# Gated weight tables kept in 32 bit, and the cast of x moved to GpSimd

## Chip, cores and metric

The kernel runs on one core of a Trainium2 chip. The metric is the device time of one execution in microseconds (us). A measurement is compared as a ratio against runs of the kernel before on the same chip.

## What is computed

The input x is 16 images of 128 channels and 32 x 32 pixels, taken as 16 batches of 1024 tokens of 128 values. Three layers follow one another:

- a 128 x 128 channel mix with the inverse of a circulant matrix;
- causal linear attention: layer norm, projections to q, k and v, `elu + 1` on q and k, 8 heads of 16, cumulative sums over the tokens, output projection, residual;
- a feed-forward layer whose weights differ from batch to batch. A small gate net turns the mean over a batch's tokens into 8 gate values g, and the weights are merged from a base and 8 task tables.

The parts that the change touches are, from the reference:

```python
gh = jax.nn.relu(jnp.einsum('bsd,hd->bsh', x, gfc1_w) + gfc1_b)
g = (jnp.einsum('bsh,eh->bse', gh, gfc2_w) + gfc2_b).mean(axis=1)
W1m = W1 + jnp.einsum('be,efd->bfd', g, tv_W1)
W2m = W2 + jnp.einsum('be,edf->bdf', g, tv_W2)
h = jax.nn.relu(jnp.einsum('bsd,bfd->bsf', x, W1m) + b1m[:, None, :])
out = jnp.einsum('bsf,bdf->bsd', h, W2m) + b2m[:, None, :]
```

## The kernel before

**Precision.** Most products run in 16 bit with split operands: a value a is stored as a_hi (a cast to f16) and a_lo (a minus a_hi, again f16), and a product is three products, hi x hi, hi x lo and lo x hi, added up in PSUM. So each 32-bit value needs a cast and a subtraction on some engine before TensorE can read it.

**Attention.** The 16 x 1024 tokens are 128 tiles of 128 tokens. All engines run the same software pipeline over slots: in slot s a stage with skew k works on tile s - k. The order of the stages in a slot is written out by hand for each engine (lines 42 to 52), and each engine runs its list in that order, waiting on semaphores. Two batches are unrolled, the others run in a loop of eight slots each (lines 429 to 447). The stages that matter here, with engine and skew:

- x_hi (ScalarE, skew 0, line 722): for the even tile n of a pair, the cast of the 256 columns of tiles n and n+1. The buffers xh and xl hold eight tiles, so the cast overwrites tiles n-8 and n-7 and first waits for their out-projections (`wo_done`).
- x_lo (GpSimd, skew 0, line 1036): the subtraction, after x_hi. In GpSimd's slot it comes after rsqrt (line 977) and z_hi (line 1020) and before z_lo, qk_hi and qk_lo.
- conv (TensorE, skew 0, line 559): needs x_hi and x_lo of its tile. Statistics on VectorE (stats1, mean_var1) follow, then rsqrt on GpSimd with skew 1, and exp_qk and v_hi on ScalarE with skew 1.
- turn_out (TensorE, skew 6, line 654) transposes the attention output after the divide on VectorE (line 907), copy_out on ScalarE brings it back, and out_project (skew 6, line 660) adds x_hi and x_lo products to it and counts `wo_done`.
- scores (skew 4) writes PSUM, scores_hi on ScalarE and scores_lo on VectorE split it, and values (TensorE, skew 5, line 629) reads the split.

TensorE's slot is state, scores, conv, turn_out, values, out_project, gate (every other slot), project.

**The task tables.** tv_W1 and tv_W2 are loaded during attention in 16 shares, one for each batch, from SyncE's queue (line 486) into a small 32-bit buffer. ScalarE casts each share to tv_hi (tv_hi, line 733, four casts of 128 x 128 for each batch), VectorE makes tv_lo (line 844), and the next load waits for that (`tv_split`).

**The merges.** Merged weights of eight batches are made at a time. A bank of PSUM takes four groups; a group is three products of table parts with gate blocks and one with the base weights (lines 1189 to 1192). ScalarE or VectorE casts the bank to its high part and VectorE subtracts the low part. Eight banks of W1 for the first half of the batches are merged in the last slots of attention (merge_w1, line 685), the other eight after attention (lines 1239 to 1243), and 16 for the second half between the two halves of the FFN loop (line 1101). That is 32 banks or 128 groups.

Of the kernel before, what the change touches and what calls it, by code (L numbers as in the profile page):

```python
# [8 lines left out]
F16 = mybir.dt.float16  # L9
BF16 = mybir.dt.bfloat16  # L10
ALU = mybir.AluOpType
# [4 lines left out]
P = 128  # L16
# [13 lines left out]
GB = 8  # L30
# [52 lines left out]
def shape_constants():  # L83
# [3 lines left out]
    def put(name, a):  # L87
        k[:a.shape[0], COL[name][0]:COL[name][1]] = a
# [6 lines left out]
    put("delta", (j[:, None] % FI == np.arange(FI)[None, :]).astype(np.float32))  # L95
# [34 lines left out]
def build(nc, d):  # L130

    top = ExitStack()
    with top:
        def sb(ctx, name, shape, dt=F32):
            return ctx.enter_context(nc.sbuf_tensor(name, shape, dt))
# [25 lines left out]
        tv = [sb(top, f"tv_{s}", [P, 2, FO * C], F16) for s in ("hi", "lo")]  # L161
# [9 lines left out]
        gbf = sb(top, "gate_blocks_f32", [P, GB, FI])  # L171
        gbh = sb(top, "gate_blocks_hi", [P, B, FI], F16)
        gbl = sb(top, "gate_blocks_lo", [P, B, FI], F16)
# [208 lines left out]
        with early, ExitStack() as pa_:  # L382
# [14 lines left out]
            tvs = sb(pa_, "tv_share", [P, 2, TVW])  # L397
# [23 lines left out]
            tv_loaded = [sem(f"tv_loaded_{i}") for i in range(2)]  # L421
            tv_hi_ready, tv_split = sem("tv_hi_ready"), sem("tv_split")
# [17 lines left out]
            def run(eng, order, stages, behind=None):  # L440
# [3 lines left out]
                with eng.Fori(2, B) as b:  # L444
                    batch(stages, b)
                for b in range(B, B + 2):
                    batch(stages, b, behind)
# [4 lines left out]
            TVP = 4  # L452
            MERGE_SLOT = 4

            with nc.Block() as block:
                @block.sync
                def _(sp):
# [28 lines left out]
                    def load_tv(b, t):  # L486
                        if t not in (1, 5) or isinstance(b, int) and b + 1 == B:
                            return
                        which = t // 4
                        sp.wait_ge(ones_set, 1)  # L490
# [3 lines left out]
                    def tv_rows(b, which):  # L494
                        src = (d["L1_ffn_tv_W1"].rearrange("e (i o) d -> (e i) (o d)", i=FI),
                               d["L1_ffn_tv_W2"].rearrange("e (i o) f -> (e i) (o f)", i=FI))[which]
                        sp.dma_start(tvs[:, which, :], src[:, bass.ds(b * TVW, TVW)]).then_inc(tv_loaded[which], 16)
# [12 lines left out]
                    for which in range(2):  # L510
                        tv_rows(0, which)
# [19 lines left out]
                def _(pe):  # L531
# [153 lines left out]
                    def merge_w1(slot):  # L685
# [9 lines left out]
                        if k == 0:  # L695
                            pe.wait_ge(base_placed, 16 * 4)
                            pe.wait_ge(tv_split, TVP * B)
# [3 lines left out]
                        gh, gl = [x[:, 0:GB, :].rearrange("p b i -> p (b i)") for x in (gbh, gbl)]  # L701
# [19 lines left out]
                def _(act):  # L721
                    def split_x(b, t):
                        if t % 2 or isinstance(b, int) and TILES * b + t == 0:
                            return
                        n = TILES * b + t
                        hf, j = t // HALF, t % HALF
                        if j == 0:
                            act.wait_ge(x_loaded[hf], 16 * (b + 1))
# [4 lines left out]
                    def tv_hi(b, t):  # L733
                        if t % 2:
                            return
                        which, part = divmod(t // 2, 2)
                        act.wait_ge(ones_set, 1)
                        act.wait_ge(tv_loaded[which], 16 * (b + 1))
                        nc.scalar.activation(tv[0][:, which, bass.ds(b * TVW + part * TVW // 2, TVW // 2)],
                                             tvs[:, which, part * TVW // 2:(part + 1) * TVW // 2], ACT.Copy, scale=WS)\  # L740
                            .then_inc(tv_hi_ready, 1)

# [82 lines left out]
                    run(act, SCALAR_ORDER, {"tv_hi": tv_hi, "split_x": split_x, "read_t1": read_t1, "v_hi": v_hi,  # L825
# [5 lines left out]
                def _(dve):  # L831
# [11 lines left out]

                    def tv_lo(b, t):
                        if t % 2:
                            return
                        which, part = divmod(t // 2, 2)
                        dve.wait_ge(tv_hi_ready, TVP * b + t // 2 + 1)
                        cols = bass.ds(b * TVW + part * TVW // 2, TVW // 2)
                        nc.vector.scalar_tensor_tensor(tv[1][:, which, cols],  # L850
                                                       tvs[:, which, part * TVW // 2:(part + 1) * TVW // 2], WS,
                                                       tv[0][:, which, cols], ALU.mult, ALU.subtract).then_inc(tv_split, 1)
# [80 lines left out]
                    def merged_w1(slot):  # L933
# [5 lines left out]
                        if slot == MERGE_SLOT - 2:  # L939
# [4 lines left out]
                            nc.vector.tensor_tensor(gbf[:, :, :],  # L944
                                                    kcol("delta").unsqueeze(1).broadcast_to([P, GB, FI]),
                                                    grep[:, 0:GB].unsqueeze(2).broadcast_to([P, GB, FI]), ALU.mult)\
                                .then_inc(gb0_chain, 1)
                            dve.wait_ge(gb0_chain, 2)
                            nc.vector.tensor_copy(gbh[:, 0:GB, :], gbf[:, :, :]).then_inc(gb0_chain, 1)
                            dve.wait_ge(gb0_chain, 3)  # L950
# [528 lines left out]
```

## Time and profile before

| | us |
|---|---|
| median of 3 runs | 747.9 |
| lowest, highest run | 747.24, 750.97 |
| the profiled execution | 749.55 |
| its span (first to last instruction) | 747.8 |
| attention loop, from about | 30 |
| attention loop, to about | 480 |

The granted clock of TensorE is 0.975 of full speed on average. The profile's page gives busy time for each engine, the span in 40 slices and the costliest groups of instructions. A line of a group says: line, engine, operation, output<-inputs, shapes, count, busy time, mean duration in ns, and the idle time before it with what ended it. A line of the timeline says: start, duration, engine, line, operation. Records on one engine can overlap, because the next instruction starts to flow in before the one ahead has written its last result; for matmuls the distance from start to start tells what one costs.

### The profile page before, as it was taken

To read this page: it belongs to the slowest core of one execution; us is meant where nothing else is said; L and a number is where in the kernel's file an instruction comes from. 1 tells how busy PE (TensorE), PEld (TensorE's weight loads), DVE (VectorE), ACT (ScalarE), POOL (GpSimd) and SP (SyncE) were. 2 spreads that over 40 slices of the span, in tenths; PEclk is the share of its full clock that TensorE was granted. 3 is DMA by queue.
4 is the path that set the end of the run, shared out by engine and by line. 5 is a ranking of instruction groups with operands and counts; after the bars stand their busy time and mean duration, and the time that the engine had idled before them with its cause. 6 is when DMAs were issued, how large, how long until landed. Compare 5 with 4: busy or idle time off the path is not lost. (4 is left out here: it accounts for less than half of the span.)

```text
span 747.8 us, 38168 instructions
## 1 busy us (share of the span) xinstructions
PE 692.5 (93%) x12002; PEld 533.8 (71%) x12002; DVE 659.1 (88%) x2409; ACT 649.1 (87%) x1780; POOL 465.2 (62%) x790
## 2 busy tenths in 40 slices
PE   4898899999999999999999999888999998999993
PEld 2576677777777777777777777775777787777772
DVE  5697889999999999999999999768898977998983
ACT  4797989999999999999999999557888876888883
POOL 3686778888888888888888888421333321333333
PEclk9798999999999999999999999899999999999998
DMA  4757676666666666666666666410222211222221
GB/s 149 112 110 134 132 129 129 148 143 131 148 142 132 148 141 132 148 141 134 148 139 135 148 142 123 74 51 1 73 85 83 71 58 31 85 70 84 84 84 70
DMA packets 202485, 82.66 MB, mean 111 GB/s; under 512 B 176093, under 2 KB 189824, under 8 KB 202377
## 3 DMA queue, kind: packets, MB, share of 16 engines
q1 hardware_dynamic: 202440, 82.08, 48.3%
q8 instruction: 26, 0.43, 0.2%
q14 instruction: 19, 0.15, 0.1%
HBM read 22.79 MB, written 17.30 MB: 54 GB/s over the span
## 5 line engine op out<-in xcount | busy, mean ns | idle before, releaser
L892 DVE SCALAR_TENSOR_TENSOR scores_lo<-p_a,scores_hi 128x512 f16<-128x512 f32 x256 | 173.3, 683 | 1.7 <-ACT scores_hi L786 1.3
L786 ACT ACTIVATE scores_hi<-p_a 128x512 f16<-128x512 f32 x256 | 156.2, 611 | 9.3 <-PE p_a L623 9.3
L1010 POOL CAST qk_parts<-qk_f 128x512 f16<-128x512 f32 x128 | 78.0, 610 | 50.2 <-issue 24.9
L1442 POOL TENSOR_TENSOR ffn_rstd_shift<-ffn_rstd_shift,consts 128x4 f32<-128x4 f32 x32 | 36.5, 1142 | 109.1 <-DVE ffn_rstd_shift L1400 109.1
L984 POOL TENSOR_TENSOR stats<-stats,consts 128x2 f32<-128x2 f32 (+1 forms) x128 | 88.2, 689 | 17.9 <-DVE stats L925 13.1
L1224 PE MATMUL psb<-merged_W_of_batch,h_hi 128*128 128x128 f16 x512 | 94.5, 220 | 2.2 <-DVE h_lo L1378 1.5
L1378 DVE TENSOR_TENSOR h_lo<-h_f,h_hi 128x512 f16<-128x512 f32 x128 | 95.6, 786 | 1.1 <-ACT h_hi L1280 1.1
L1269 ACT ACTIVATE h_f<-psb,merged_b_of_batch 128x512 f32<-128x512 f32 x128 | 87.2, 709 | 10.3 <-PE psb L1205 8.6
L1225 PE MATMUL psb<-merged_W_of_batch,h_hi 128*128 128x128 f16 x512 | 94.2, 220 | 0.0
L1226 PE MATMUL psb<-merged_W_of_batch,h_lo 128*128 128x128 f16 x512 | 94.1, 220 | 0.0
L1016 POOL TENSOR_TENSOR qk_parts<-qk_f,qk_parts 128x256 f16<-128x256 f32 x128 | 85.9, 671 | 10.2
L640 PE MATMUL p_o<-v_parts,scores_hi 128*128 128x17 f16 x1024 | 90.3, 171 | 1.8 <-issue 0.2
L640 PEld LDWEIGHTS p_o<-v_parts,scores_hi 128*128 128x128 f16 x1024 | 82.1, 96 | 12.4 <-issue 11.7
L644 PE MATMUL p_o<-v_parts,scores_lo 128*128 128x17 f16 x1024 | 89.8, 171 | 0.0
L642 PE MATMUL p_o<-v_parts,scores_hi 128*128 128x16 f16 x1024 | 89.6, 170 | 0.0
L642 PEld LDWEIGHTS p_o<-v_parts,scores_hi 128*128 128x128 f16 x1024 | 80.5, 96 | 1.0
L644 PEld LDWEIGHTS p_o<-v_parts,scores_lo 128*128 128x128 f16 x1024 | 80.1, 96 | 0.0
L1435 POOL TENSOR_TENSOR normed<-normed,ln_gain_rows 128x512 f32<-128x512 f32 x32 | 40.6, 1268 | 59.5 <-ACT normed L1289 59.5
L1289 ACT ACTIVATE normed<-psb,ffn_rstd_shift 128x128 f32<-128x128 f32 x128 | 48.1, 456 | 33.8 <-DVE ffn_rstd_shift L1406 33.8
L801 ACT ACTIVATE z<-t,stats 128x128 f32<-128x128 f32 x128 | 65.5, 512 | 0.9 <-DVE stats L875 0.9
L765 ACT ACTIVATE exp_qk<-p_in,stats 128x256 f32<-128x256 f32 x128 | 60.8, 475 | 3.7 <-POOL stats L984 2.1
L616 PE MATMUL p_a<-mask_factors_bf 64*128 64x256 bf16 x512 | 60.2, 277 | 3.5 <-DVE scores_lo L892 1.2
(215 smaller groups left out, 2697.5 us busy)
## 6 DMA issues: line engine op xcount, KB each, us to landing
x_f<-in_x SPq DMA_DIRECT2D x32, 256.0 KB, 3.2
t_rows<-t SPq DMA_DIRECT2D x64, 128.0 KB, 1.8
t_back<-t_rows SPq DMA_DIRECT2D x32, 256.0 KB, 2.6
out<-out_tile SPq DMA_DIRECT2D x32, 256.0 KB, 2.1
tv_share<-in_L_ffn_tv_W SPq DMA_DIRECT2D x32, 128.0 KB, 2.2
qkT_parts<-qk_parts SPq DMA_TRANSPOSE x128, 3.1
zT_hi_lo<-z_parts SPq DMA_TRANSPOSE x128, 2.3
merged_W<-in_L_ffn_W SPq DMA_DIRECT2D x2, 256.0 KB, 4.4
```

The lines of the kernel that those rows point to most:

```text
L640: mm(num[:, h, :], hi, vp[:, t, h, 0:VW], start=(h == 0), stop=False, skip_group_check=True)
L642: mm(num[:, h, 0:DH], hi, vp[:, t, h, VW:VW + DH], start=False, stop=False, skip_group_check=True)
L644: last = mm(num[:, h, :], lo, vp[:, t, h, 0:VW], start=False, stop=True, skip_group_check=True)
L786: nc.scalar.activation(ah[:, t % 2, cols], p_a[:, cols], ACT.Relu).then_inc(ahi_ready[eo], 1)
L892: nc.vector.scalar_tensor_tensor(al[:, t % 2, cols], p_a[:, cols], 0.0, ah[:, t % 2, cols], ALU.max, ALU.subtract).then_inc(alo_ready[eo], 1)
L984: nc.gpsimd.tensor_tensor(s[:, :, RSTD], s[:, :, VAR], mhalf[:, 0:2 if both else 1], ALU.pow)\
L1016: nc.gpsimd.tensor_tensor(parts_at(t, 2 * DH, 0, [[1, DH]]), qk[:, t % 4, :].rearrange("p (w h i) -> p w h i", h=NH, i=DH), pk[:, t % 4, : ...
L1224: mm(o, hi, w2b[:, bb, 0, c, :], start=False, stop=False)
L1225: mm(o, hi, w2b[:, bb, 1, c, :], start=False, stop=False)
L1226: last = mm(o, lo, w2b[:, bb, 0, c, :], start=False, stop=(c == FC - 1))
L1269: nc.scalar.activation(hf_[:, c, :], ps[:, c, :], ACT.Relu, bias=b1s[:, h // 2, c:c + 1], scale=1.0 / WS).then_inc(h_ready[c], 1)
L1378: nc.vector.tensor_tensor(hl[:, h % 2, c, :], hf_[:, c, :], hh[:, h % 2, c, :], ALU.subtract)\
```

## The change

The task tables are kept in 32 bit. The load writes them straight into their final place (tv), so tv_hi and tv_lo and their semaphores go, and so do the high and low parts of the gate blocks. A group of the merge becomes one 32-bit product and the base product. The factor WS that the casts applied goes into the constant "delta".

The cast x_hi moves from ScalarE to GpSimd with skew -1, that is, it stands in the slot ahead of the tile's own, as the last item of that slot. Its waits are the same. x_lo (the old split_x of GpSimd) now comes right after rsqrt, ahead of z_hi. turn_out moves ahead of conv in TensorE's order. ScalarE's and VectorE's orders are rearranged. GpSimd's loop ends one batch earlier, and the last batch is written out. Both table loads of a batch go out in one slot.

```diff
-TENSOR_ORDER = [("state", 3), ("scores", 4), ("conv", 0), ("turn_out", 6), ("values", 5), ("out_project", 6),
+TENSOR_ORDER = [("state", 3), ("scores", 4), ("turn_out", 6), ("conv", 0), ("values", 5), ("out_project", 6),
                 ("gate", 13), ("project", 0)]
-SCALAR_ORDER = [("normalise", 10), ("split_x", 0), ("relu_qk", 2), ("read_t1", 7), ("gate_relu", 14),
-                ("exp_qk", 1), ("state_hi", 3), ("v_hi", 1), ("tv_hi", 0), ("scores_hi_0", 4), ("copy_out", 6),
-                ("scores_hi_1", 4)]
-VECTOR_ORDER = [("shift2", 9), ("divide", 6), ("make_qk", 2), ("v_lo", 2), ("stats2", 7), ("stats1", 0),
-                ("state_lo", 3), ("mean_var1", 0), ("mean_var2", 7), ("scores_lo_0", 4), ("denominator", 5),
-                ("scores_lo_1", 4), ("tv_lo", 1), ("invert", 5)]
-GPSIMD_ORDER = [("rsqrt", 1), ("z_hi", 10), ("split_x", 0), ("z_lo", 10), ("qk_hi", 2), ("qk_lo", 2),
+SCALAR_ORDER = [("relu_qk", 2), ("normalise", 10), ("gate_relu", 14), ("read_t1", 7), ("exp_qk", 1),
+                ("state_hi", 3), ("v_hi", 1), ("copy_out", 6), ("scores_hi_0", 4), ("scores_hi_1", 4)]
+VECTOR_ORDER = [("shift2", 9), ("divide", 6), ("make_qk", 2), ("stats2", 7), ("v_lo", 2), ("stats1", 0),
+                ("mean_var2", 7), ("state_lo", 3), ("mean_var1", 0), ("scores_lo_0", 4), ("denominator", 5),
+                ("scores_lo_1", 4), ("invert", 5)]
+GPSIMD_ORDER = [("rsqrt", 1), ("x_lo", 0), ("z_hi", 10), ("z_lo", 10), ("qk_hi", 2), ("qk_lo", 2), ("x_hi", -1),
                 ("last_rsqrt2", 8)]
...
-                        sp.wait_ge(tv_split, TVP * b + TVP // 2 * (which + 1))
-                        tv_rows(b + 1, which)
+                        tv_rows(b + 1)
...
-                            th, tl = tv[0][:, 0, c0:c0 + P], tv[1][:, 0, c0:c0 + P]
-                            mm(o, th, gh, start=True, stop=False)
-                            mm(o, th, gl, start=False, stop=False)
-                            mm(o, tl, gh, start=False, stop=False)
+                            mm(o, tv[:, 0, c0:c0 + P], g, start=True, stop=False)
                             last = mm(o, w1s[:, c0:c0 + P], delta2h[:, :, :].rearrange("p b i -> p (b i)"),
                                       start=False, stop=True)
...
-                        at_least(act, wo_done, n - TILES + 2)
-                        cols = slice(j * P, (j + 2) * P)
-                        nc.scalar.activation(xh[:, hf, cols], xf[:, hf, cols], ACT.Copy).then_inc(xh_ready, 1)
...
+                    def x_hi(b, t):
+                        if t % 2 or isinstance(b, int) and TILES * b + t == 0:
+                            return
+                        n = TILES * b + t
+                        hf, j = t // HALF, t % HALF
+                        loaded, used = 16 * (b + 1), n - TILES + 2
+                        if not isinstance(n, int):
+                            loaded, used = pool.to_reg(loaded), pool.to_reg(used)
+                        pool.wait_ge(ones_set, 1)
+                        if j == 0:
+                            pool.wait_ge(x_loaded[hf], loaded)
+                        at_least(pool, wo_done, used)
+                        cols = slice(j * P, (j + 2) * P)
+                        nc.gpsimd.tensor_copy(xh[:, hf, cols], xf[:, hf, cols]).then_inc(xh_ready, 1)
...
-                                mm(o, th[:, c0:c0 + P], gh, start=True, stop=False)
-                                mm(o, th[:, c0:c0 + P], gl, start=False, stop=False)
-                                mm(o, tl[:, c0:c0 + P], gh, start=False, stop=False)
+                                mm(o, rows[:, c0:c0 + P], gb[:, g * GB:(g + 1) * GB, :].rearrange("p b i -> p (b i)"),
+                                   start=True, stop=False)
```

## Rows read from the trace of the kernel before

**Rows 1.** Busy time by stretch: stretch, PE, PEld, DVE, ACT, POOL busy, PEclk, DMA, GB/s.

```profile
196.00:420.00 224.00, 215.32 (x4519) 166.20 (x4517) 216.69 (x859) 222.17 (x699) 189.66 (x354) 1.00 0.65 141
482.00:495.00 13.00, 11.59 (x148) 9.78 (x146) 8.76 (x19) 6.78 (x20) 3.94 (x11) 0.91 0.19 47
495.80:505.00 9.20, 9.13 (x143) 8.70 (x144) 5.85 (x15) 4.18 (x7) 1.13 (x3) 1.00 0.21 61
606.90:621.40 14.50, 14.50 (x259) 14.36 (x257) 9.84 (x16) 10.61 (x19) 1.27 (x1) 1.00 0.06 20
```

**Rows 2.** Instructions grouped by line, attention loop from 196 to 420 us.

```profile
L984 POOL TENSOR_TENSOR stats<-stats,consts 128x2 f32<-128x2 f32 x65 | 45.3, 696 | 3.1 <-DVE stats L925 3.1
L1010 POOL CAST qk_parts<-qk_f 128x512 f16<-128x512 f32 x64 | 39.0, 610 | 22.8 <-issue 11.0 <-DVE qk_f L869 9.1 <-PE p_a L623 2.7
L1042 POOL TENSOR_TENSOR x_lo<-x_f,x_hi 128x256 f16<-128x256 f32 x32 | 23.2, 725 | 0.8
L1028 POOL CAST z_parts<-z 128x128 f16<-128x128 f32 x65 | 18.8, 289 | 0.0
L850 DVE SCALAR_TENSOR_TENSOR tv_lo<-tv_share,tv_hi 128x128 f32 x32 | 16.3, 508 | 0.0
L731 ACT ACTIVATE x_hi<-x_f 128x256 f16<-128x256 f32 x32 | 13.4, 418 | 0.1
L739 ACT ACTIVATE tv_hi<-tv_share 128x128 f32 x32 | 10.8, 338 | 0.0
```

**Rows 3.** TensorE in order of time, one pair of slots: start, duration, line.

```profile
247.85 0.22 PE L665 MATMUL p_m<-w_in_hi,x_hi 128*128 128x128 f16 x1
...
248.01 0.44 PE L669 MATMUL p_m<-w_outT,attn_outT 128*128 128x128 f32 x2
...
250.07 0.23 PE L567 MATMUL p_m<-w_in_hi,x_hi 128*128 128x128 f16 x1 [0.22 <-POOL x_lo L1042]
...
250.54 0.17 PE L640 MATMUL p_o<-v_parts,scores_hi 128*128 128x17 f16 x1
...
254.70 0.22 PE L665 MATMUL p_m<-w_in_hi,x_hi 128*128 128x128 f16 x1
...
254.87 0.44 PE L669 MATMUL p_m<-w_outT,attn_outT 128*128 128x128 f32 x2
255.14 0.33 PE L580 MATMUL p_in<-w_in_hi,x_hi 128*128 128x384 f16 x1
```

**Rows 4.** ScalarE and GpSimd in order of time, the same pair.

```profile
248.15 0.70 POOL L984 TENSOR_TENSOR stats<-stats,consts 128x2 f32<-128x2 f32 x1
...
248.49 0.42 ACT L731 ACTIVATE x_hi<-x_f 128x256 f16<-128x256 f32 x1
248.80 0.29 POOL L1028 CAST z_parts<-z 128x128 f16<-128x128 f32 x1
248.81 0.43 ACT L772 ACTIVATE p_in<-p_in,stats 128x256 f32<-128x256 f32 x1
...
249.05 0.79 POOL L1042 TENSOR_TENSOR x_lo<-x_f,x_hi 128x256 f16<-128x256 f32 x1
```

**Rows 5.** TensorE in order of time, a pair of the other kind.

```profile
268.63 0.22 PE L665 MATMUL p_m<-w_in_hi,x_hi 128*128 128x128 f16 x1
...
270.68 0.23 PE L567 MATMUL p_m<-w_in_hi,x_hi 128*128 128x128 f16 x1
...
271.25 0.33 PE L658 MATMUL p_m<-consts,attn_out 128*128 128x128 f32 x1 [0.23 <-DVE attn_out L911]
271.57 0.18 PE L640 MATMUL p_o<-v_parts,scores_hi 128*128 128x17 f16 x1
...
275.77 0.22 PE L665 MATMUL p_m<-w_in_hi,x_hi 128*128 128x128 f16 x1
```

**Rows 6.** TensorE in order of time, one group of the merge between the FFN halves.

```profile
609.00 0.22 PE L1189 MATMUL psb<-gate_blocks_hi,tv_hi 128*128 128x128 f16 x1
...
609.16 0.22 PE L1192 MATMUL psb<-delta_f,W_hi_lo_rows 128*128 128x128 f16 x1
```

More of the change, by code:

```diff
@@ L94, in shape_constants @@
     put("blk", (j[:, None] // 64 == np.arange(2 * VW)[None, :] // VW).astype(np.float32))
-    put("delta", (j[:, None] % FI == np.arange(FI)[None, :]).astype(np.float32))
+    put("delta", WS * (j[:, None] % FI == np.arange(FI)[None, :]).astype(np.float32))
     put("delta2", np.vstack([np.eye(FI), np.eye(FI)]))
@@ L160, in build @@
         lnb = sb(top, "ln_bias_col", [P, 1])
-        tv = [sb(top, f"tv_{s}", [P, 2, FO * C], F16) for s in ("hi", "lo")]
+        tv = sb(top, "tv", [P, 2, FO * C])
         w1s = sb(top, "W1_hi_lo_rows", [P, FO * C], F16)
@@ L420, in build @@
             qk_turned, z_turned = [[sem(f"{s}_{i}") for i in range(4)] for s in ("qk_turned", "z_turned")]
-            tv_loaded = [sem(f"tv_loaded_{i}") for i in range(2)]
-            tv_hi_ready, tv_split = sem("tv_hi_ready"), sem("tv_split")
+            tv_loaded = sem("tv_loaded")
             def at_least(eng, s, value):
@@ L438, in batch, with run @@
                         behind(TILES * (b - B) + slot)
-            def run(eng, order, stages, behind=None):
+            def run(eng, order, stages, behind=None, upto=B):
                 stages = [(skew, stages[name]) for name, skew in order]
@@ L443, in run @@
                     batch(stages, b)
-                with eng.Fori(2, B) as b:
+                with eng.Fori(2, upto) as b:
                     batch(stages, b)
-                for b in range(B, B + 2):
-                    batch(stages, b, behind)
+                for b in range(upto, B + 2):
+                    batch(stages, b, behind if b >= B else None)
             MEAN, VAR, RSTD, SHIFT = 9, 10, 11, 12
@@ L451, in build @@
             NW1 = GB
-            TVP = 4
             MERGE_SLOT = 4
@@ L486, in load_tv, with tv_rows @@
                     def load_tv(b, t):
-                        if t not in (1, 5) or isinstance(b, int) and b + 1 == B:
+                        if t != 1 or isinstance(b, int) and b + 1 == B:
                             return
-                        which = t // 4
-                        sp.wait_ge(ones_set, 1)
-                        sp.wait_ge(tv_split, TVP * b + TVP // 2 * (which + 1))
-                        tv_rows(b + 1, which)
[L494 to L497, printed above, removed]
+                        tv_rows(b + 1)
+                    def tv_rows(b):
+                        cols = bass.ds(b * TVW, TVW)
+                        for i, src in enumerate((d["L1_ffn_tv_W1"].rearrange("e (i o) d -> (e i) (o d)", i=FI),
+                                                 d["L1_ffn_tv_W2"].rearrange("e (i o) f -> (e i) (o f)", i=FI))):
+                            sp.dma_start(tv[:, i, cols], src[:, cols]).then_inc(tv_loaded, 16)
                     def store(b, t):
@@ L508, in store @@
                             .then_inc(t1_stored[pair], 16)
-                    for which in range(2):
-                        tv_rows(0, which)
+                    tv_rows(0)
                     sp.wait_ge(base_stored, 32)
@@ L696, in merge_w1 @@
                             pe.wait_ge(base_placed, 16 * 4)
-                            pe.wait_ge(tv_split, TVP * B)
+                            pe.wait_ge(tv_loaded, 32 * B)
                             pe.wait_ge(gb0_ready, 1)
@@ L700, in merge_w1 @@
                             pe.wait_ge(mlo_ready, k - 1)
-                        gh, gl = [x[:, 0:GB, :].rearrange("p b i -> p (b i)") for x in (gbh, gbl)]
+                        g = gb[:, 0:GB, :].rearrange("p b i -> p (b i)")
                         for j in range(4):
@@ L823, in merged_w1_hi @@
                             .then_inc(mhi_ready, 1)
-                    run(act, SCALAR_ORDER, {"tv_hi": tv_hi, "split_x": split_x, "read_t1": read_t1, "v_hi": v_hi,
+                    run(act, SCALAR_ORDER, {"read_t1": read_t1, "v_hi": v_hi,
                         "exp_qk": exp_qk, "relu_qk": relu_qk,
@@ L842, in mean_var1 @@
                         nc.vector.bn_aggr(st[:, t % 4, MEAN:MEAN + 2], st[:, t % 4, 0:9]).then_inc(mv1, 1)
[L844 to L852, printed above, removed]
                     def v_lo(b, t):
@@ L964, in merged_w1 @@
                         nc.vector.tensor_tensor(lo, src, hi, ALU.subtract).then_inc(mlo_ready, 1)
-                    run(dve, VECTOR_ORDER, {"tv_lo": tv_lo, "stats1": stats1, "mean_var1": mean_var1, "v_lo": v_lo,
+                    run(dve, VECTOR_ORDER, {"stats1": stats1, "mean_var1": mean_var1, "v_lo": v_lo,
                         "make_qk": make_qk, "shift2": shift2, "state_lo": state_lo,
@@ L1045, in _ @@
                     run(pool, GPSIMD_ORDER, {"rsqrt": rsqrt, "qk_lo": qk_lo,
-                        "split_x": split_x,
-                        "last_rsqrt2": last_rsqrt2, "qk_hi": qk_hi, "z_hi": z_hi, "z_lo": z_lo})
+                        "x_hi": x_hi, "x_lo": x_lo,
+                        "last_rsqrt2": last_rsqrt2, "qk_hi": qk_hi, "z_hi": z_hi, "z_lo": z_lo}, upto=B - 1)
         with ExitStack() as pb:
```

42 lines of the change are left out of this document (7 added, 35 removed).

## The prediction

> **What bounds the kernel now.** I first cut the span into stretches and read who is busy in each [rows 1]. In the attention loop (here 196 to 420 us) four engines are nearly full: ScalarE 222 of 224 us, VectorE 217, TensorE 215, GpSimd 190. Such a table does not say which one sets the pace, because records on one engine overlap their neighbours. The other three stretches are the merges of the gated weights: at the end of attention (482 to 495), after it (495.8 to 505) and between the two FFN halves (606.9 to 621.4). In the last TensorE is busy for the whole 14.5 us, the other engines are not: there TensorE alone sets the time.
>
> Next I read the attention loop grouped by line [rows 2]: x_hi is cast 32 times in these 224 us, so one pair of slots takes 7.00 us; these rows also hold the durations of all that is moved.
>
> Then I followed one pair in order of time, on TensorE [rows 3] and on ScalarE and GpSimd [rows 4]. The out-projection of an odd slot starts at 247.85 and ends at 248.45 (248.01 + 0.44), and x_hi, which overwrites what it read, starts at 248.49: released by it, 0.04 behind. x_lo runs from 249.05 to 249.84 on GpSimd, and the convolution (L567), which waits for x_lo, starts at 250.07. Values start at 250.54 and the next odd slot's out-projection at 254.70. So there is a closed loop over TensorE, ScalarE, GpSimd and TensorE again: 2.22 us from out-projection to convolution, 0.47 to values, 4.16 of TensorE's in-order work to the next one, 6.85 in all. The neighbouring kind of pair [rows 5] has 2.05, 0.89 (turn_out waited for the divide on VectorE) and 4.20: 7.14. Their mean is 2.14 + 0.68 + 4.18 = 7.00, the period that the count gave. I take this loop, not ScalarE's load, as the bound of attention.
>
> **The cast of x on GpSimd.** It is placed a slot ahead, but its release is not: x_hi for tiles n and n+1 waits for the out-projection of tile n-7, which is in slot n-1, the slot in which the cast now stands, as the last item. So it is let go by the very event that lets it go now. Behind it on GpSimd's in-order queue stand rsqrt and then x_lo. Before, rsqrt ran while TensorE was still projecting (248.15 to 248.85 in [rows 4]); now it stands between the two halves of the split. The stretch from out-projection to convolution becomes:
> - out-projection start to end: 0.60 [rows 3].
> - Release: 0.04 for ScalarE, 0.24 from x_lo to TensorE (249.84 to 250.07). I take 0.10.
> - The cast, 128x256: no row shows it on GpSimd. Bounds are 128x128 in 0.289 and 128x512 in 0.610 [rows 2]; in between by size it is 0.40, and I take 0.37 until rsqrt starts, since records on GpSimd overlap by some 0.03 to 0.05.
> - rsqrt until the next starts: 0.65 (248.15 to 248.80).
> - x_lo: its mean is 0.725, stretched when tv_lo runs beside it (0.79 in the pair shown), and tv_lo goes. I take 0.68.
> - x_lo to convolution: 0.24.
>
> Sum 2.64, against 2.14: +0.50 a pair. Ends: 2.47 with the cheap cast and the short release, 3.06 with the dear ones and x_lo at its old mean.
>
> **The new order on TensorE.** turn_out moves ahead of the convolution, so its wait for the divide falls into the time in which the convolution would wait anyway, and 0.1 us of transposing leaves the stretch to values. What stays there is three convolution products (0.06 apart) and the waits of values, which are gone through one by one after a stall: 0.47 in [rows 3] with turn_out. I take 0.40; ends 0.18 (no wait exposed) and 0.47. Against 0.68: -0.28. The 4.18 stays. New pair: 2.64 + 0.40 + 4.18 = 7.22, +0.22. The wait exists for n of 8 and more, 60 pairs: +13 us. Ends: 6.83 (-10 us) and 7.71 (+43).
>
> **What is taken off ScalarE and VectorE.** x_hi holds ScalarE for 0.32 (248.49 to 248.81, [rows 4]) and tv_hi for at most 0.34, tv_lo holds VectorE for 0.51 on average [rows 2]. None lies on the loop except x_hi, whose successor is counted above; the divide that tv_lo delayed is counted at turn_out. I cost the rest at nothing: the loop hides it. The room pays for this: rsqrt now ends about 0.8 later (248.45 + 0.10 + 0.37 + 0.70 = 249.62 instead of 248.85), so exp and v_hi, which wait for it on ScalarE with scores_hi behind them, may start as much later. The freed 0.66 covers most of that; without this cover scores_lo on VectorE would be late next (rival 4). On GpSimd qk_hi and qk_lo are also late by the cast and x_lo; its busy 5.9 us a pair become 6.3, under 7.2.
>
> **Queues.** SyncE loses its waits for tv_split, and both tv loads of a batch go out in one slot instead of two; its transposes of q and k stand ahead of them and are wanted two slots on. Nothing. GpSimd's last batch in straight code, and a cast and a subtraction less for the gate blocks: nothing, they stand beside the waits for the merge.
>
> **The merges.** 128 times three 16-bit products become one 32-bit product. The three take 0.167 (609.00 to 609.16, [rows 6]). A 128x128 32-bit product stands in the loop: L669 takes two records each, and from its start to the next product it is 0.27 (254.87 to 255.14, [rows 3]). So +0.107 each. Between the FFN halves TensorE is full: 64 x 0.107 = 6.8. After attention it is nearly full (9.13 of 9.20): 32 x 0.107 = 3.4. At the end of attention TensorE is idle for 1.4 of 13 us, at a granted clock of 0.91 of full speed, waiting for VectorE between banks: of 3.4 I take 2.4. Together +12.6; ends 6 (half the price, tail hidden) and 14.
>
> By the Trainium skill (page "FP8 and Floating Point Precision", section TensorE Precision Notes) a true 32-bit product is four passes through the array. At 0.056 a pass that is an estimate of 0.22, and by it the merges would cost 6.7 instead of 12.6. The trace's 0.27 differs, and I go by the trace.
>
> **Sum.** The profiled execution took 749.55 us, a span of 747.8 and 1.75 around it. 749.55 + 13 + 12.6 = 775.2. It stands 1.65 over the median of the runs, 747.9, so against the median: 773.
>
> **Rivals.**
> 1. Faster: ScalarE's load is the bound. For it: 222 of 224 us busy. Then 0.66 less a pair is up to -40 us; TensorE's own busy time (215) would stop it at -0.27 a pair, -16, though a busy TensorE is not one at its peak. Between them -28, with the merges -15: 732. It decides if the new x_hi starts before out-projection has ended, or the cast hardly costs. Against it: the loop above adds up to the whole period, and x_hi starts 0.04 after its release. 12%.
> By the Trainium skill (page "Perfetto Trace Analysis", section Identifying the Most-Contended Engine) occupancy picks the engine to relieve first, and this would be that rival. The trace's loop speaks against it.
> 2. No change: the stretch to values shrinks to 0.18 and the cast is cheap, -10, and the merges give it back: about 750. 8%.
> 3. Attention does not move, as if the loop had slack that I don't see; only the merges are paid: 760. 20%.
> 4. Worse: GpSimd becomes the bound behind the wait. Its wait for out-projection holds rsqrt, then exp, scores_hi and scores_lo, and the next scores start late, or the cast is 0.61: 7.7 a pair, +43 and +14: 805. 10%.
> 5. My forecast, 762 to 790: 50%.
>
> **Numbers.** A measurement of this kernel can tell about 0.5% (3.7 us) from no change. Faster is rival 1, same is rival 2, slower the other three: 0.12, 0.08, 0.80. From 750 to 790 leaves out rival 1 and most of rival 4. Within my forecast alone it would be 762 to 790.
>
> **What would show it.** Right: in the attention loop x_hi on GpSimd starts some 0.1 behind L669's end, rsqrt and x_lo follow it with no gap, the convolution of even slots waits for x_lo, pairs take about 7.2, ScalarE and VectorE show idle time; a merge bank (four groups) takes 4 x (0.27 + 0.06) = 1.3 us instead of 4 x 4 x 0.056 = 0.89. Wrong: pairs under 7.0 with TensorE hardly waiting at the convolution, GpSimd never waiting ahead of x_hi, or 32-bit products closer than 0.25 to their successors.

## The result and the profile after

The changed kernel took 772.51 us (median of 4 runs, 772.09 to 772.75) against 748.91 for the kernel before on the same chip (747.24 to 750.97): a ratio of 1.031, 95% interval 1.028 to 1.034. The profiled execution took 772.75 with a span of 771.0.

Read along the timeline, the 23.2 us that the span grew came at these places:

| up to | before, us | after, us | added |
|---|---|---|---|
| end of the last out-projection | 485.1 | 497.3 | +12.2 |
| start of the last merge product in the last slots | 493.8 | 507.8 | +1.8 |
| first product of the FFN (merges after attention done) | 504.9 | 522.4 | +3.5 |
| start of the merges between the FFN halves | 607.0 | 624.1 | -0.4 |
| first product of the second FFN half | 623.4 | 647.4 | +6.9 |
| end | 747.8 | 771.0 | -0.8 |

So about half is attention and half the merges. The busy time by stretch (start and end, length, then TensorE's products (PE) and its weight loads (PEld), VectorE (DVE), ScalarE (ACT), GpSimd (POOL), granted clock, DMA share, GB/s), for the four stretches of [rows 1]:

```profile
196.00:420.00 224.00, 212.78 (x4384) 164.84 (x4382) 200.45 (x800) 200.83 (x614) 190.85 (x374) 1.00 0.63 136
494.50:507.50 13.00, 12.61 (x110) 11.42 (x109) 7.97 (x18) 6.03 (x17) 3.90 (x10) 0.97 0.20 48
509.70:522.30 12.60, 12.52 (x110) 11.73 (x110) 6.08 (x15) 4.19 (x7) 1.13 (x3) 1.00 0.14 43
624.00:645.40 21.40, 21.40 (x195) 20.50 (x192) 10.42 (x16) 10.72 (x19) 1.27 (x1) 1.00 0.04 13
```

In the attention loop ScalarE fell from 222 to 201 us busy and VectorE from 217 to 200, and yet the loop became slower. An engine that gets idle time while the kernel slows down was not the one to relieve. In the last stretch TensorE is still busy for every microsecond, for 21.4 us instead of 14.5, with fewer instructions (195 instead of 259): what is left costs more.

The groups by line for the attention loop, which answer to [rows 2] (count, busy, mean ns, idle before and its releaser):

```profile
L936 POOL TENSOR_TENSOR stats<-stats,consts 128x2 f32<-128x2 f32 x63 | 44.0, 698 | 1.2 <-issue 0.5
...
L732 ACT ACTIVATE exp_qk<-p_in,stats 128x256 f32<-128x256 f32 x62 | 29.5, 476 | 15.0 <-POOL stats L936 15.0
...
L1009 POOL TENSOR_TENSOR x_lo<-x_f,x_hi 128x256 f16<-128x256 f32 x31 | 20.8, 671 | 0.0
...
L1001 POOL CAST x_hi<-x_f 128x256 f16<-128x256 f32 x32 | 12.7, 397 | 22.8 <-PE p_m L660 22.8
```

The cast costs GpSimd 0.397 us, and ahead of it GpSimd stands still for 0.71 us each time (22.8 / 32), let go by the out-projection (L660). Behind it rsqrt (L936) is late, and exp on ScalarE waits for that: its idle time. x_lo has become shorter, 0.671 instead of 0.725: tv_lo is gone, and in tables_alone below, which also leaves it out, x_lo takes 0.669.

One pair in order of time, TensorE, which answers to [rows 3] (start, duration, line):

```profile
260.05 0.22 PE L656 MATMUL p_m<-w_in_hi,x_hi 128*128 128x128 f16 x1
...
260.21 0.44 PE L660 MATMUL p_m<-w_outT,attn_outT 128*128 128x128 f32 x2
...
262.74 0.23 PE L558 MATMUL p_m<-w_in_hi,x_hi 128*128 128x128 f16 x1 [0.24 <-POOL x_lo L1009]
...
267.21 0.22 PE L656 MATMUL p_m<-w_in_hi,x_hi 128*128 128x128 f16 x1
```

The values of this pair (L631) start at 263.21. And GpSimd in the same pair, which answers to [rows 4]:

```profile
260.81 0.40 POOL L1001 CAST x_hi<-x_f 128x256 f16<-128x256 f32 x1 [0.78 <-PE p_m L660]
261.17 0.70 POOL L936 TENSOR_TENSOR stats<-stats,consts 128x2 f32<-128x2 f32 x1
261.83 0.67 POOL L1009 TENSOR_TENSOR x_lo<-x_f,x_hi 128x256 f16<-128x256 f32 x1
```

The out-projection ends at 260.65, the cast starts 0.16 behind it, rsqrt follows after 0.36, x_lo after 0.66, and the convolution starts 0.24 behind x_lo's end. "A slot ahead" is true of the place in the list, not of the time: the cast is let go by the same event as before, and rsqrt now stands between the two halves of the split. Over 36 pairs the means are 2.69 us from out-projection to convolution, 0.37 to values, 4.15 to the next out-projection: 7.21.

A group of the merge between the FFN halves, which answers to [rows 6]:

```profile
626.67 0.44 PE L1154 MATMUL psb<-gate_blocks,tv 128*128 128x128 f32 x2
626.95 0.22 PE L1156 MATMUL psb<-delta_f,W_hi_lo_rows 128*128 128x128 f16 x1
627.01 0.44 PE L1154 MATMUL psb<-gate_blocks,tv 128*128 128x128 f32 x2
```

From one group to the next it is 0.34 by these rounded times (0.332 in the mean), of which the 32-bit product takes 0.28; before, four products 0.056 apart made 0.223.

### The profile page after: what moved, and what is told of

Same layout as the page of the kernel before. It is cut to its first block and busy times, and to the rows that moved or that the text cites. A ratio compares the mean times of both kernels' runs of the same rounds, so it can differ in the third digit from the quotient of the medians.

```text
span 771.0 us, 37564 instructions
## 1 busy us (share of the span) xinstructions
PE 714.2 (93%) x11874; PEld 553.0 (72%) x11874; DVE 640.2 (83%) x2341; ACT 618.1 (80%) x1653; POOL 480.4 (62%) x853
## 5 line engine op out<-in xcount | busy, mean ns | idle before, releaser
L753 ACT ACTIVATE scores_hi<-p_a 128x512 f16<-128x512 f32 x256 | 139.4, 606 | 0.7 <-PE p_a L614 0.7
L936 POOL TENSOR_TENSOR stats<-stats,consts 128x2 f32<-128x2 f32 (+1 forms) x128 | 88.3, 690 | 9.9 <-DVE stats L809 7.8
L631 PE MATMUL p_o<-v_parts,scores_hi 128*128 128x17 f16 x1024 | 90.3, 171 | 2.0
L631 PEld LDWEIGHTS p_o<-v_parts,scores_hi 128*128 128x128 f16 x1024 | 81.6, 96 | 11.0 <-issue 8.8
L802 DVE BATCH_NORM_STATS2 stats<-p_m 128x6 f32<-128x128 f32 x128 | 38.4, 300 | 51.7 <-PE p_m L560 51.3
L607 PE MATMUL p_a<-mask_factors_bf 64*128 64x256 bf16 x512 | 66.6, 280 | 7.0 <-DVE scores_lo L849 4.9
```

What stands on the lines that cost most here:

```text
L631: mm(num[:, h, :], hi, vp[:, t, h, 0:VW], start=(h == 0), stop=False, skip_group_check=True)
L753: nc.scalar.activation(ah[:, t % 2, cols], p_a[:, cols], ACT.Relu).then_inc(ahi_ready[eo], 1)
L936: nc.gpsimd.tensor_tensor(s[:, :, RSTD], s[:, :, VAR], mhalf[:, 0:2 if both else 1], ALU.pow)\
```

## The experiments

Two theories go into all of them. **The loop**: attention is paced by the closed loop out-projection, x_hi, x_lo, convolution, values, out-projection, and the change made it longer by putting the cast on GpSimd, with rsqrt behind it, between out-projection and x_lo. **The load**: an engine's amount of work paces it. "Pair" is the mean time of two slots, "end" that of the last out-projection; both are from the trace. The kernel before ran beside each: 746.65 us for the first four kernels, 748.35 for the next four, 747.04 for the last four, and 748.91 beside the changed kernel. The ratios are taken within a group; a difference of times across groups is good to about 2 us.

| kernel | median us | ratio | 95% | pair | end |
|---|---|---|---|---|---|
| cast_alone | 762.04 | 1.020 | 1.018 to 1.022 | 7.24 | 499.3 |
| tables_alone | 755.49 | 1.011 | 1.008 to 1.014 | 6.98 | 481.3 |
| rsqrt_first | 760.00 | 1.018 | 1.017 to 1.020 | 6.98 | 484.3 |
| cast_on_scalar | 757.18 | 1.014 | 1.012 to 1.016 | 6.98 | 482.3 |
| cast_twice | 804.43 | 1.077 | 1.074 to 1.080 | 7.67 | 527.0 |
| scalar_load | 772.89 | 1.034 | 1.032 to 1.037 | 7.21 | 495.1 |
| turn_out_behind_conv | 787.40 | 1.053 | 1.047 to 1.059 | 7.57 | 513.6 |
| orders_alone | 778.74 | 1.042 | 1.039 to 1.044 | 7.54 | 515.3 |
| before_fewer_stores | 747.36 | 0.9995 | 0.998 to 1.001 | 6.98 | 482.8 |
| after_fewer_stores | 770.89 | 1.032 | 1.031 to 1.034 | 7.21 | 496.7 |
| scalar_fewer_stores | 752.26 | 1.006 | 1.004 to 1.008 | 6.85 | 478.6 |
| split_fewer_stores | 739.89 | 0.989 | 0.987 to 0.992 | 6.84 | 477.2 |

**cast_alone** keeps the split tables and the 16-bit merges of before, and moves the cast with the new orders (tv_hi and tv_lo stay in them):

```diff
-GPSIMD_ORDER = [("rsqrt", 1), ("z_hi", 10), ("split_x", 0), ("z_lo", 10), ("qk_hi", 2), ("qk_lo", 2),
+GPSIMD_ORDER = [("rsqrt", 1), ("x_lo", 0), ("z_hi", 10), ("z_lo", 10), ("qk_hi", 2), ("qk_lo", 2), ("x_hi", -1),
```

> The move of x_hi and the new orders alone: tables split in 16 bit on ScalarE and VectorE as before (tv_hi behind v_hi, tv_lo ahead of invert), merges with three products as before. Loop theory: attention as in the changed kernel, 7.2 to 7.3 a pair against 6.98, +13 to +17 us; merges as before: 762 to 766 where the kernel before takes 749. Rival, the relief of ScalarE and VectorE pays for part of the move: then taking it back costs more, 770 and over.

It took 762.04, as expected. The pair is 7.24 (2.72, 0.36, 4.15), and with attention 14.2 us longer and nothing paid in the merges the time rises by 15.4. The loss in attention comes from the cast and its orders; the tables have no part in it.

**tables_alone** is the other half: 32-bit tables and merges, the cast on ScalarE, the orders of before without tv_hi and tv_lo.

```diff
-                 ("exp_qk", 1), ("state_hi", 3), ("v_hi", 1), ("tv_hi", 0), ("scores_hi_0", 4), ("copy_out", 6),
+                 ("exp_qk", 1), ("state_hi", 3), ("v_hi", 1), ("scores_hi_0", 4), ("copy_out", 6),
...
-                ("scores_lo_1", 4), ("tv_lo", 1), ("invert", 5)]
+                ("scores_lo_1", 4), ("invert", 5)]
```

> The 32-bit tables and merges alone: x_hi on ScalarE and all orders as before, without tv_hi and tv_lo. Loop theory: merges +12 us; in attention x_lo is not stretched (0.67 for 0.73) and the divide is not late behind tv_lo (0.68 to values becomes about 0.48), so a pair takes 6.75 instead of 6.98, -14 us: about 747. Rival, ScalarE's load is the bound: 0.34 less a pair, -20 us, and +12: 741. If tv_hi and tv_lo cost nothing at all: 761.

755.49, between the two figures: the merges cost their 12 us, attention ended 3.8 us earlier, but the pair stayed at 6.98. The loop had got room, for the convolution now started 0.44 us behind x_lo instead of 0.24. It waited for something else.

**rsqrt_first** is the changed kernel with one thing turned round: x_hi stands in its own slot, behind rsqrt.

```diff
-GPSIMD_ORDER = [("rsqrt", 1), ("x_lo", 0), ("z_hi", 10), ("z_lo", 10), ("qk_hi", 2), ("qk_lo", 2), ("x_hi", -1),
+GPSIMD_ORDER = [("rsqrt", 1), ("x_hi", 0), ("x_lo", 0), ("z_hi", 10), ("z_lo", 10), ("qk_hi", 2), ("qk_lo", 2),
```

> The changed kernel with the cast x_hi moved from the end of GpSimd's slot to the place right behind rsqrt of the next slot (skew 0); nothing is added or left out. Loop theory: rsqrt runs again while TensorE is still in the out-projection, so the stretch from out-projection to convolution loses rsqrt: 0.60 + 0.15 + 0.40 + 0.08 + 0.67 + 0.24 = 2.14 instead of 2.69; with 0.37 and 4.15 a pair takes 6.66 instead of 7.21, 60 pairs, -33 us: about 739 (731 to 748 if the next limit comes sooner). Rival, the cast's own load on GpSimd or the loss of a faster caster is the cost: GpSimd does the same work, so 772.

760.00: 12.5 us better than the changed kernel, so rsqrt between cast and subtraction is what attention lost by. But it fell short of what was expected. The pair is 6.98, again with room behind x_lo (0.48).

**cast_on_scalar** keeps all of the change but puts the cast back on ScalarE:

```diff
-SCALAR_ORDER = [("relu_qk", 2), ("normalise", 10), ("gate_relu", 14), ("read_t1", 7), ("exp_qk", 1),
+SCALAR_ORDER = [("normalise", 10), ("x_hi", 0), ("relu_qk", 2), ("gate_relu", 14), ("read_t1", 7), ("exp_qk", 1),
```

> The changed kernel with x_hi back on ScalarE at skew 0, second in its slot; tables, merges and all other orders as changed. Loop theory: 0.60 + 0.08 + 0.42 + 0.10 + 0.67 + 0.24 = 2.11 from out-projection to convolution, 6.63 a pair, -35 us: about 738. Rival, GpSimd's load: its 0.4 us a pair comes off, -24 us: 748. If ScalarE's load were the bound, the cast back on it would cost time: 772 or more.

757.18, some 19 us over what was expected. The pair is 6.98 for the third time, with 0.56 behind x_lo. Three kernels with different loops and one period: a second limit must lie at 6.98. It is taken up below.

**cast_twice** doubles the suspected cost: a second cast on GpSimd into a spare tile, ahead of x_hi.

```diff
+                        nc.gpsimd.tensor_copy(spare[:, :], xf[:, hf, cols])
                         nc.gpsimd.tensor_copy(xh[:, hf, cols], xf[:, hf, cols]).then_inc(xh_ready, 1)
```

> The changed kernel with a second cast of the same 128x256 columns into a spare tile on GpSimd, behind the same wait and ahead of the real one; its output is not used. Loop theory: the cast lies on the loop, so a pair takes 0.36 to 0.40 longer, 60 pairs, +22 to +24 us: about 795. Rival, the move costs by GpSimd's total load, which has nearly a microsecond a pair to spare: 772 to 775.

804.43, 32 us over the changed kernel, some 9 more than expected. GpSimd in one pair, in order of time:

```profile
258.86 0.40 POOL L1002 CAST spare<-x_f 128x256 f16<-128x256 f32 x1 [0.65 <-PE p_m L661]
259.19 0.40 POOL L1003 CAST x_hi<-x_f 128x256 f16<-128x256 f32 x1
259.56 0.70 POOL L937 TENSOR_TENSOR stats<-stats,consts 128x2 f32<-128x2 f32 x1
260.22 0.67 POOL L1011 TENSOR_TENSOR x_lo<-x_f,x_hi 128x256 f16<-128x256 f32 x1
```

The out-projection lets the spare cast go, all the rest follows by as much later, and the stretch from out-projection to convolution grew from 2.69 to 2.99: 18 us in 60 pairs, somewhat less than expected. Most of the other 14 us come from the clock. The stretch from values to the next out-projection is 4.15 in the mean, as in the changed kernel, but for six pairs between 110 and 470 us, where it is 5.5 to 5.7. In each of them TensorE's granted clock is at the lower of its two levels, 1.2 GHz instead of 2.4, for 3.4 us. The busy time of one such stretch (its clock stands behind the five engines), and two of its products:

```profile
262.50:265.90 3.40, 3.40 (x36) 2.21 (x36) 2.21 (x9) 2.35 (x8) 2.99 (x6) 0.50 0.54 109
```

```profile
263.56 0.53 PE L572 MATMUL p_in<-w_in_hi,x_hi 128*128 128x384 f16 x1
263.88 0.53 PE L573 MATMUL p_in<-w_in_lo,x_hi 128*128 128x384 f16 x1
```

They are 0.32 apart; the same two are 0.16 apart in the changed kernel (260.49 and 260.65). Such a pair takes some 9.05 instead of 7.51, so six cost 9 us; the last 5 us of the 32 are not accounted for. The kernel before and the changed kernel have no such stretch between 110 and 470 us. It is not only the profiled execution: the four runs of cast_twice had a mean clock of 0.958 to 0.969, those of the changed kernel 0.983 to 0.986. Ahead of each of the six falls TensorE had stood still for 0.58 to 0.62 us at the convolution (at most 0.43 in the changed kernel), but 29 other stands of 0.57 to 0.65 had no fall behind them; why the clock fell is open.

**scalar_load** gives ScalarE a useless 128x256 cast for each pair.

```diff
+                    def extra(b, t):
+                        if t % 2 == 0:
+                            nc.scalar.activation(spare[:, :], kc[:, 0:2 * P], ACT.Copy)
```

> The changed kernel with one more cast of 128x256 on ScalarE in each pair, of constants into a spare tile that nothing reads, where x_hi used to stand. Loop theory: ScalarE lies off the loop and idles about 10% of attention: 772 to 774. Rival, ScalarE's load sets the pace: 0.32 us a pair, +19 us: 791.

772.89, no difference from 772.51, as the loop has it. By line in the attention loop:

```profile
L737 ACT ACTIVATE exp_qk<-p_in,stats 128x256 f32<-128x256 f32 x62 | 29.4, 475 | 6.2 <-POOL stats L941 6.2
...
L713 ACT ACTIVATE spare<-consts 128x256 f16<-128x256 f32 x31 | 13.4, 431 | 0.0
```

The extra work took the idle time ahead of exp, which fell from 15.0 to 6.2 us. By the Trainium skill (page "Perfetto Trace Analysis", section Identifying the Most-Contended Engine) the engine with the highest occupancy is the one to relieve first; the measurement goes against it for this kernel: ScalarE was the busiest, but the change took 21 us from it without a gain, and giving 9 back cost nothing.

**turn_out_behind_conv** is the changed kernel with TensorE's old order.

```diff
-TENSOR_ORDER = [("state", 3), ("scores", 4), ("turn_out", 6), ("conv", 0), ("values", 5), ("out_project", 6),
+TENSOR_ORDER = [("state", 3), ("scores", 4), ("conv", 0), ("turn_out", 6), ("values", 5), ("out_project", 6),
```

> The changed kernel with TensorE's old order, turn_out behind the convolution. Loop theory: turn_out comes back into the stretch from convolution to values, 0.12 us and its wait steps after the stall, 0.37 becomes 0.49 to 0.6: +7 to +14 us: 779 to 786. Rival, the order does not matter because turn_out waits for the divide anyway: 772.

787.40, 14.9 us over the changed kernel and 1.4 over the expected range. The stretch from convolution to values is 0.51 instead of 0.37. At full clock the stretch behind it is 4.12 instead of 4.15, so a pair takes 7.31 instead of 7.21: 6 us in 60 pairs is what the new order is worth to the loop. The mean of 7.57 in the table has seven pairs in it, between 110 and 470 us, that take 8.8 to 9.15 since the clock is halved for 3.4 us in each, as in cast_twice:

```profile
253.80:257.20 3.40, 3.40 (x37) 2.08 (x35) 2.39 (x9) 2.60 (x9) 2.81 (x6) 0.51 0.58 117
```

At 1.5 us each they add 10 us, and the two together are the 16.3 us by which attention ends later. The mean clock of its four runs was 0.962 to 0.975. Whether the order itself brings the lower clock is not shown.

**orders_alone** is the kernel before with only the new orders: tables split, cast on ScalarE, tv_hi ahead of copy_out, tv_lo ahead of invert.

```diff
-TENSOR_ORDER = [("state", 3), ("scores", 4), ("conv", 0), ("turn_out", 6), ("values", 5), ("out_project", 6),
+TENSOR_ORDER = [("state", 3), ("scores", 4), ("turn_out", 6), ("conv", 0), ("values", 5), ("out_project", 6),
```

> The kernel before with the new orders only: x_hi on ScalarE, tables split as before, turn_out ahead of the convolution, x_lo right behind rsqrt. Loop theory: 2.11 to 2.18 + 0.40 + 4.15 = 6.66 to 6.73 a pair, -15 to -19 us, merges as before: 730 to 734 where the kernel before takes 749. Rival, ScalarE and VectorE are too full for it (99% and 97% busy before): 745 to 750.

778.74, a plain miss. Waits in the attention loop, then VectorE and TensorE at one boundary of slots:

```profile
PE p_m L657 <- DVE attn_out L910: 12.7, 30, 0.5
...
ACT attn_outT L777 <- PE p_m L657: 10.4, 31, 0.6
```

```profile
258.21 0.76 DVE L849 SCALAR_TENSOR_TENSOR tv_lo<-tv_share,tv_hi 128x128 f32 x1
258.89 0.19 DVE L904 RECIPROCAL denominators<-denominators 128x8 f32<-128x8 f32 x1
...
259.11 0.29 DVE L910 TENSOR_TENSOR attn_out<-p_o,denominators 128x128 f32<-128x128 f32 x1
```

```profile
259.46 0.33 PE L657 MATMUL p_m<-consts,attn_out 128*128 128x128 f32 x1 [0.42 <-DVE attn_out L910]
259.75 0.23 PE L566 MATMUL p_m<-w_in_hi,x_hi 128*128 128x128 f16 x1
```

Two of its pairs fall to half the clock as well; without them the pair is 7.46. tv_lo puts off the divide by 0.68, turn_out waits for the divide, and the convolution, now behind turn_out, waits with it, though x_lo is long done (0.94 to 1.14 us earlier). So turn_out ahead of the convolution helps only if the divide is early or x_lo late anyway. The changed kernel has both. In cast_on_scalar x_lo is early too, and there tv_lo is missing: the pair is 6.98 instead of 7.54. split_fewer_stores below moves tv_lo alone among the orders.

**The limit at 6.98.** In tables_alone, waits of the attention loop show one that the kernel before hardly has (0.2 us in all):

```profile
PEld p_a L615 <- DMA qkT_parts<-qk_parts: 14.1, 24, 0.7
PE p_a L615 <- DMA qkT_parts<-qk_parts: 7.1, 21, 0.5
```

Scores wait for the transposed q and k. rsqrt_first and cast_on_scalar have the same wait (7.4 and 7.8 us on PEld). SyncE's queue in cast_on_scalar, in order of time:

```profile
273.42 1.17 SPq L476 DMA_TRANSPOSE zT_hi_lo<-z_parts  x1
274.79 1.23 SPq L467 DMA_TRANSPOSE qkT_parts<-qk_parts  x1
276.30 0.36 SPq L498 DMA_DIRECT2D t_rows<-t  x1
276.94 1.18 SPq L476 DMA_TRANSPOSE zT_hi_lo<-z_parts  x1
278.33 1.24 SPq L467 DMA_TRANSPOSE qkT_parts<-qk_parts  x1
279.76 1.17 SPq L476 DMA_TRANSPOSE zT_hi_lo<-z_parts  x1
```

Each issue follows the one ahead after about 0.2 to 0.3 us, without a wait; only once in a batch is there a gap over 0.4, of 0.58. The queue has no room left: sixteen transposes at 1.2, two loads of x, four stores and the table loads take 27.93 us for a batch of eight slots, 6.98 a pair. The page of the kernel before does not count this as busy. By the Trainium skill (page "Perfetto Trace Analysis", section What "DMA-bound" means) a solid track of DMA slices on the issuing engine's sequencer is one of the things that a kernel can be bound on. The track here comes close to that, with gaps of 0.24 us in the mean between issues; whether it binds is for the next experiments.

But the kernel before issues as densely: its loads of x are 28.00 us apart, and its loop measures 27.92 (next experiment). So the loop could be its bound, or the queue. The stores of t are easily merged: two of four tiles for a batch instead of four of two.

```diff
-                        if t % 2 == 0:
+                        if t % HALF < HALF - 1:
                             return
...
-                        sp.dma_start(d["t1"][bass.ds((2 * b + hf) * P, P), 2 * C * i:2 * C * (i + 1)],
-                                     yt[:, 2 * pair:2 * pair + 2, :].rearrange("p a c -> p (a c)"))\
-                            .then_inc(t1_stored[pair], 16)
+                        sp.dma_start(d["t1"][bass.ds((2 * b + hf) * P, P), 0:HALF * C],
+                                     yt[:, HALF * hf:HALF * (hf + 1), :].rearrange("p a c -> p (a c)"))\
+                            .then_inc(t1_stored[2 * hf], 16)
```

This edit was made in four kernels. **before_fewer_stores**, the kernel before with it:

> The kernel before with the stores of t merged, two of four tiles a batch instead of four of two tiles. A store holds SyncE's queue for 0.35 us and 0.26 of gap, so the queue, which is full at 28.0 us a batch, would need 26.8. If the loop over TensorE, ScalarE and GpSimd binds the kernel before (my theory), a pair stays at 6.98 and the time at 747 to 750. If SyncE's queue is what holds it at 28.0 us a batch (rival), a pair falls towards 6.70: 730 to 735.

747.36 against 747.04: no change. SyncE's queue now has 32 gaps over 0.35 us in the window instead of 8, and the pair is still 6.98, with the convolution 0.24 behind x_lo in every kind of pair. The loop bound the kernel before, with the queue just beside it, and issues without gaps were no proof that the queue bound it.

**after_fewer_stores**, the changed kernel with it:

> The changed kernel with the stores merged in the same way. Its batches take 28.87 us, 0.9 more than SyncE's queue needs in the other kernels. Loop theory: nothing, 771 to 774. If the queue's gaps or the transposes behind the stores count here too: down by up to 1.2 us a batch, 755.

770.89, a ratio of 1.032 where the changed kernel had 1.031, and a pair of 7.21: no change. The changed kernel too is bound by its loop.

**scalar_fewer_stores**, cast_on_scalar with it:

> cast_on_scalar (32-bit tables, x_hi on ScalarE, the new orders) with the stores merged. In it the convolution starts 0.56 us behind x_lo instead of 0.24, scores wait for the transposes, and SyncE's queue has no gaps: theory is that the queue binds there at 27.93 us a batch. Then the queue needs 26.7 and a pair falls to 6.68 to 6.75: 738 to 744. If something else holds 6.98 in all of these kernels: 756 to 759.

752.26: the ratio falls from 1.014 to 1.006, some 6 us, and the pair to 6.85. The wait of scores for the transposes is gone, and now the queue waits (SyncE's waits in the attention loop):

```profile
SPq L475 <- POOL z_parts L995: 4.5, 8, 0.6
```

So the queue was the limit at 6.98 there. For tables_alone and rsqrt_first, which were not run with merged stores, that is inferred from the same wait and the same period. The next limit came sooner than expected. In the busy time of this kernel's attention loop TensorE is at 220, and ScalarE at 220 as well:

```profile
196.00:420.00 224.00, 220.34 (x4599) 173.61 (x4598) 211.36 (x843) 219.83 (x678) 191.21 (x361) 1.00 0.66 144
```

In the list of waits nothing stands ahead of TensorE's products but 1.8 us of scores_lo. It may be TensorE's own work in order, but ScalarE is as full; neither was tried, and what holds the pair at 6.85 is open.

**split_fewer_stores** is orders_alone with the stores merged and tv_lo moved:

```diff
-VECTOR_ORDER = [("shift2", 9), ("divide", 6), ("make_qk", 2), ("stats2", 7), ("v_lo", 2), ("stats1", 0),
+VECTOR_ORDER = [("shift2", 9), ("divide", 6), ("make_qk", 2), ("stats2", 7), ("v_lo", 2), ("tv_lo", 1), ("stats1", 0),
...
-                ("scores_lo_1", 4), ("tv_lo", 1), ("invert", 5)]
+                ("scores_lo_1", 4), ("invert", 5)]
```

> orders_alone (the split tables and 16-bit merges of before, x_hi on ScalarE, the new orders) with tv_lo moved on VectorE from just ahead of invert and divide to just ahead of stats1, and the stores merged. If tv_lo ahead of divide was what made orders_alone slow, and the queue is the limit behind it, a pair takes 6.70 to 6.85 and the merges cost what they do in the kernel before: 727 to 738. If tv_lo was the cause but the queue has no say: 745 to 748. If tv_lo was not the cause: 770 to 779.

739.89: 1.1% faster than the kernel before (0.987 to 0.992) and some 32 us faster than the changed one, 2 us over the range expected. Nearly 39 us came back from orders_alone, and merged stores alone gave about 6 in cast_on_scalar, so the place of tv_lo is most of it by inference; the two edits were not run apart. It keeps the cheap merges, and the pair is 6.84.

## Why the prediction was right

- **The loop as the bound.** Right. before_fewer_stores and after_fewer_stores took work from the nearest other candidate, SyncE's queue, and nothing moved; scalar_load and cast_twice put the same kind of work once beside the loop and once into it, and the first cost nothing, the second 0.30 us a pair, 18 of its 32 us (the clock took most of the others). rsqrt_first shows which part of the loop the change paid for.
- **The cast.** Out-projection to convolution was put at 2.64 and measured 2.69 in the mean: the cast until rsqrt 0.40 (taken 0.37), release 0.15 (0.10), rsqrt 0.66 (0.65), x_lo 0.67 (0.68), x_lo to convolution 0.20 (0.24). The small errors have both signs and cancel in part. The reason given for x_lo was too simple: in the kernel before tv_lo runs beside x_lo in every pair, and x_lo is stretched only where tv_lo started first (see the last section).
- **The new order on TensorE.** Put at 0.40, measured 0.37. That the wait for the divide would fall into the wait for x_lo was right; turn_out_behind_conv shows 0.51 without it.
- **Attention in all.** A pair of 7.22 was predicted, 7.21 measured; +13 us predicted, +12.2 measured to the last out-projection.
- **What was costed at nothing.** The cover named was the 0.66 us freed on ScalarE. It was not needed to that extent: exp does wait for the later rsqrt (15.0 us in 224), but scalar_load used up part of the room and the time stayed.
- **The merges.** 0.107 for each group was predicted and 0.109 measured (0.332 less 0.223). Between the FFN halves 6.8 against 6.9; after attention 3.4 against 3.5; in the last slots 2.4 against 1.8. The estimate of 0.22 from the Trainium skill (page "FP8 and Floating Point Precision", section TensorE Precision Notes: four passes) is not what this shape takes: 0.275 to the next product.
- **Rivals.** Rival 1 (ScalarE's load) fell with scalar_load, rival 2 (a cheap cast and no exposed wait) with the 2.69 and 0.37 measured, rival 3 (slack in the loop) with cast_alone. Rival 4's mechanism, late rsqrt making scores late, shows in no run: even in cast_twice, with rsqrt later by another cast, the stretch from values to the next out-projection stays at 4.15 at full clock.

What the prediction did not see is that its loop had hardly any room below it. Rival 1 let TensorE's own busy time stop the gain. SyncE's queue, set at "nothing", would have stopped it at 6.98 at once. This is correct for the change as it was made, and the queue's limit is why three of the kernels that I tried first (rsqrt_first, cast_on_scalar, tables_alone) gave 12 to 17 us against the changed kernel, where 25 to 35 were expected; the merged stores show it for cast_on_scalar.

## What to carry to other kernels

Moving a stage earlier in an engine's list brings nothing if its release does not move: find the event that lets it go, then read what the stage now holds up behind it on an in-order engine. Before undoing a loop's cost, ask for the next limit, the issuing queue of the transfers too, which the count of busy engines leaves out. A queue whose issues follow each other without gaps has no room left, but only taking work from it tells whether it binds: nothing moved in the kernel before, 6 us in cast_on_scalar. Before a difference of times is given to a mechanism, compare the granted clock, pair by pair: it made some 10 us of the differences in cast_twice and turn_out_behind_conv. And an order that is good with one set of stages can be bad with one stage more, as tv_lo ahead of the divide was.

## What was not expected of the hardware

- A transpose on SyncE's queue holds it for 1.17 us (z) or 1.23 us (q and k), and the next issue starts about 0.2 us later; a plain store of 128 KB or load of 256 KB holds it for 0.35. Sixteen transposes, with the 0.2 behind each, fill some 22 of the 28 us of a batch.
- Beside each other, x_lo on GpSimd and tv_lo on VectorE do not share the delay: the one that starts second pays it. In the kernel before, over 48 pairs between 130 and 460 us, tv_lo starts first in 24 and takes 0.28, and x_lo then takes 0.77 to 0.80, as at 249.05 in [rows 4]; in the other 24 x_lo starts first and takes 0.67, and tv_lo takes 0.67 to 0.80 and ends 0.15 behind x_lo. In orders_alone x_lo is first in every pair, so tv_lo takes 0.70 in the mean. One pair of each order from the kernel before:

```profile
249.02 0.28 DVE L850 SCALAR_TENSOR_TENSOR tv_lo<-tv_share,tv_hi 128x128 f32 x1
...
262.75 0.67 POOL L1042 TENSOR_TENSOR x_lo<-x_f,x_hi 128x256 f16<-128x256 f32 x1
262.89 0.68 DVE L850 SCALAR_TENSOR_TENSOR tv_lo<-tv_share,tv_hi 128x128 f32 x1
```

- TensorE's granted clock fell to its lower level for 3.4 us at a time inside the attention loop of cast_twice (six times between 110 and 470 us) and turn_out_behind_conv (seven), and never in that stretch of the kernel before or the changed kernel. One fall costs a pair 1.5 us.
- A cast of 128x256 from 32 to 16 bit takes GpSimd 0.397 us, not longer than ScalarE's 0.418 for the same cast [rows 2].
